# Moving the projection and norm of one batch row's context into the cross attention of the pair before, and taking the zero products out of it

## What is computed

```python
x = x + self_attention(layernorm(x))       # 16 heads, 4 key heads, rotary q and k
x = x + cross_attention(layernorm(x), ctx) # ctx: 361 rows of 256, the last 16 apart
x = x + mixture(layernorm(x))              # shared expert + 4 of 60 experts per token
```

## Time and profile before

| what | us |
|---|---|
| median of three runs | 1265.41 |
| the profiled execution's own time | 1263.68 |
| its span, first to last instruction | 1261.6 |
| TensorE busy in the span | 1135.0 (90%) |
| GpSimd busy | 395.0 (31%) |
| VectorE busy | 495.9 (39%) |
| ScalarE busy | 254.8 (20%) |
| records of the zero products: 320, busy | 67.3 |

### The profile page before, as it was taken

One profiled execution on the slowest core, in us unless ns is written; L12 is line 12 of the kernel. 1 busy time (PEld: TensorE's weight loads), 2 busy tenths in 40 slices (PEclk: granted clock), 3 DMA queues, 4 the chain that ended last, 5 costly groups with the idle time before them and its releaser, 6 DMA issues.

```text
span 1261.6 us, 19386 instructions
## 1 busy us (share of the span) xinstructions
PE 1135.0 (90%) x5710; PEld 626.4 (50%) x5710; DVE 495.9 (39%) x1360; ACT 254.8 (20%) x796; POOL 395.0 (31%) x917
## 2 busy tenths in 40 slices
PE   1889899898998989989897999999898998989898
PEld 0444574445654456544474655554454544445454
DVE  7242765426754267542474560121121211212144
ACT  0141331413414134141341200011110111111100
POOL 3677304874048740486400046000000000000062
PEclk9899899998999989999898999999998998989999
DMA  9999001000010000100202488399999999999653
GB/s 317 342 395 366 11 2 54 23 1 1 1 55 2 22 1 2 55 1 1 90 1 74 122 291 288 121 331 386 382 390 395 399 392 392 391 389 397 243 149 104
DMA packets 76439, 232.73 MB, mean 184 GB/s; under 512 B 11346, under 2 KB 13750, under 8 KB 68670
## 3 DMA queue, kind: packets, MB, share of 16 engines
q1 hardware_dynamic: 58686, 197.55, 42.7%
q10 hardware_dynamic: 11520, 20.98, 4.6%
q0 software_dynamic: 6144, 13.13, 3.5%
HBM read 178.40 MB, written 53.22 MB: 184 GB/s over the span
## 4 chain that ended last, share of the span: by engine, by line
PE 49%; POOL 19%; issue 11%; DMA 9%; DVE 6%; SPq 2%; POOLq 2%; ACT 1%; DVEq 0%; ACTq 0%
PE ps L1080 10%; PE ps L1147 7%; DMA arena<-in_w 7%; PE ps L1143 6%; PE ps L1241 5%; POOL arena L684 4%; PE ps L809 4%; PE ps L1178 3%; PE ps L1174 3%; PE ps L964 3%; POOL arena L681 2%; POOL arena L706 2%; PE ps L944 2%; POOL arena L695 2%; POOL arena L697 2%
## 5 line engine op out<-in xcount | busy, mean ns | idle before, releaser
L809 PE MATMUL ps<-arena 128*100 128x512 f32 (+3 forms) x576 | 223.1, 540 | 4.4 <-ACT arena L1263 3.7
L756 POOL DMA_INDIRECT arena<-ys_d,slot_u x32 | 33.1, 1034 | 426.7 <-issue 418.6
L809 PEld LDWEIGHTS ps<-arena 128*100 128x100 f32 (+1 forms) x576 | 91.0, 178 | 113.4 <-issue 107.6
L1147 PE MATMUL ps<-arena 128*64 128x352 f32 x640 | 113.5, 514 | 25.4 <-issue 16.1
L1080 PE MATMUL ps<-arena 128*128 128x400 f32 x352 | 121.8, 508 | 6.9 <-DMA arena<-xT_d 6.0
L1914 DVE COPY arena<-ps 128x512 f32<-128x512 f32 x40 | 27.7, 692 | 225.8 <-PE ps L1135 225.8
L891 PE MATMUL ps<-arena 128*100 128x512 f32 x256 | 114.5, 592 | 0.0
L1143 PE MATMUL ps<-arena 128*128 128x352 f32 x320 | 98.0, 459 | 0.8 <-issue 0.8
L1080 PEld LDWEIGHTS ps<-arena 128*128 128x128 f32 x352 | 67.8, 194 | 59.5 <-issue 8.5
L1316 ACT ACTIVATE arena<-ps,arena 100x345 f32<-100x345 f32 x128 | 69.2, 546 | 113.9 <-DVE arena L1714 112.2
L1147 PEld LDWEIGHTS ps<-arena 128*64 128x64 f32 x640 | 53.1, 152 | 78.1 <-issue 59.7
(11 more groups left out here) (214 smaller groups left out, 1513.2 us busy)
## 6 DMA issues: line engine op xcount, KB each, us to landing
arena<-in_w SPq DMA_DIRECT2D x60, 1408.0 KB, 11.8
arena<-in_w SPq DMA_DIRECT2D x60, 512.0 KB, 12.9
xs_d<-zero SPq DMA_DIRECT2D x5, 3328.0 KB, 26.2
arena<-in_w SPq DMA_DIRECT2D x60, 192.0 KB, 13.4
arena<-xs_d ACTq DMA_DIRECT2D x40, 256.0 KB, 7.4
ys_d<-arena ACTq DMA_DIRECT2D x40, 256.0 KB, 7.2
ys_d<-zero SPq DMA_DIRECT2D x2, 3328.0 KB, 24.4
arena<-in_se_up SPq DMA_DIRECT2D x11, 512.0 KB, 6.7
```

The costliest lines, as they stand in the source:

```text
L809: last = nc.tensor.matmul(ps[0:m, k, 0:cols[1] - cols[0]], lhs(c), w[:, c, cols[0]:cols[1]], start=(c == 0), stop=(c == n_c - 1))
L1147: last = nc.tensor.matmul(ps[half * HALF:(half + 1) * HALF, 3 + gu, 0:I], xsT[1][:, c, half * HALF:(half + 1) * HALF], w13_s[s][1 + half][ ...
```

## The change

The first context's six products and three key norms for pair i+1 now run in pair i's steps; those of pair 0 run in the preamble. The zero products are gone (`STEP_ZEROS` holds (0, 0) for every step).

- TensorE: keys `kx(0, c)` in steps 1, 2 and 4, values `vx(0, c)` in steps 6, 7 and 8 (four records each). The first part begins with the three key transposes of the first context and keeps three units (those of j = 1), spread in a new order; `transpose_probs(1)` and `values(1, 0)` now stand behind the last part of `attend_out(0)`.
- VectorE: evictions of the same products in those steps, `rotate` cut in two, the reciprocals of the first row taken one by one between, `probs_T(1)` put behind three pieces of the layer norm that follows the first residual.
- GpSimd: norm of unit (1, 0) first, then the probabilities of j = 0, then the two residual sums; one norm, the probabilities of j = 1, one norm, blocks, bias, the query norms, and last the three norms of the next pair's first context (not in the last pair, which is now code of its own behind a loop of three).
- The spread of the reciprocal sums moves from GpSimd to ScalarE, into the buffer `t0`.
- SP: the first context of pair i+1 is loaded at the start of pair i, the second where both were.
- Preamble: six products, six evictions and three head norms on VectorE; the pairs begin when the six banks are free.

```diff
+STEP_HOOKS = {0: [("xq", 1)], 1: [("kx", 0, 0)], 2: [("kx", 0, 1)], 3: [("xqT", 1)], 4: [("kx", 0, 2), ("ds", 1)],
+              5: [("dpT", 0), ("rx", 0)], 6: [("vx", 0, 0), ("xo", 0)], 7: [("vx", 0, 1)], 8: [("dpT", 1)]}
+STEP_ZEROS = {t: (0, 0) for t in range(1, 9)}
...
             sp.dma_start(w_kv, Wkv.rearrange("(c p) n -> p c n", p=P)).then_inc(w_loaded["w_kv"], 16)
+            load_context(0, 0)
...
+                sp.wait_ge(first_full, 2 * LN_)
+                sp.wait_ge(full[6].sem, full[6].before(i))
+                load_context(min(i + 1, PAIRS - 1), 0)
...
+                head_norm((1, 0))
                 normalise(0)
-                head_norm(NORMS[2])
+                first_residual(0)
+                first_residual(1)
+                head_norm((1, 1))
                 normalise(1)
-                for n in range(3, 6):
-                    head_norm(NORMS[n])
+                head_norm((1, 2))
+                dca_blocks(0)
                 add_bias(0)
-                head_norm(NORMS[6])
-                head_norm(NORMS[7])
+                head_norm(("q", 0))
+                dca_blocks(1)
                 add_bias(1)
+                head_norm(("q", 1))
+                if more:
+                    for c in range(LN_):
+                        head_norm((0, c))
...
+            pe.wait_ge(kv_centred, 1)
+            pe.wait_ge(c_loaded[0], 16)
+            for c in range(LN_):
+                for n, bank_ in ((0, c), (1, (3, 5, 6)[c])):
+                    for a in range(CC):
+                        last = nc.tensor.matmul(ps[0:LC, bank_, :], c_in[0][:, a, c * LC:(c + 1) * LC], w_kv[:, a, n * D:(n + 1) * D],
+                                                start=(a == 0), stop=(a == CC - 1))
+                    last.then_inc(first_full, 1)
...
+            pe.wait_ge(first_free, 2 * LN_)
...
                 transpose_x("xT3", 3, 1)
-                kv_project(0, between=lambda: gate(1))
+                for c in range(LN_):
+                    key_transpose(0, c)
+                context_project("kx", 1, 0)
+                gate(1)
+                transpose_qk(0)
+                context_project("vx", 1, 0)
+                scores(0)
                 self_project(1)
...
                 attend_out(0, 2)
-                values(1, 0)
+                context_project("kx", 1, 2)
+                context_project("vx", 1, 1)
                 begin("o", 0)
                 end(attend_out(0, 3), "o", 0)
+                transpose_probs(1)
+                values(1, 0)
                 values(1, 1)
...
                     if 1 <= t <= FOURS:
-                        keep_busy(t // 6, 2)
+                        keep_busy(t // 6, STEP_ZEROS[t][0])
                         four_transposes(t - 1, 2)
-                        keep_busy(t // 6, 3)
+                        keep_busy(t // 6, STEP_ZEROS[t][1])
+                    if t == FOURS:
+                        context_project("vx", 0, 2)
...
+            for c in range(LN_):
+                key = hn[NORMS.index((0, c)) % 3][0:LC, :]
+                head_norm(key, key, LC, 1.0).then_inc(hn_ready.sem, 1)
...
                 residual("o", 0)
                 dve.wait_ge(xn_stored[0], i * 16 + 1)
                 dve.wait_ge(x1_ready, i * 2 + 2)
                 wait_normed((2, 0))
-                run(norm_x(0))
+                after_o = norm_x(0)
+                for _ in range(3):
+                    next(after_o)
+                probs_T(1)
+                run(after_o)
                 query(0)
+                context_value(1, 2)
```

More of the change, by code:

```diff
@@ L57, with __init__ @@
     all = []
-    def __init__(self, sem, keys):
-        self.sem, self.keys = sem, list(keys)
+    def __init__(self, sem, keys, head=0):
+        self.sem, self.keys, self.head = sem, list(keys), head
         Signal.all.append(self)
     def at(self, i, key):
-        return i * len(self.keys) + (self.keys.index(key) + 2)
+        return i * len(self.keys) + (self.keys.index(key) + 2 + self.head)
     def before(self, i):
-        return i * len(self.keys) + 1
+        return i * len(self.keys) + (1 + self.head)
     def prior(self, i, key):
-        return i * len(self.keys) + (self.keys.index(key) + 1)
-KV_UNITS = [(j, c) for c in range(LN_) for j in range(2)]
+        return i * len(self.keys) + (self.keys.index(key) + 1 + self.head)
 FOURS = 2 * H // 4
@@ L646, in _, with pair, first_residual @@
             pool.wait_ge(kd_ready, 1)
-            with pool.Fori(0, PAIRS) as i:
-                for j in range(2):
+            def pair(i, more):
+                def first_residual(j):
                     pool.wait_ge(x_loaded[j], i * 16 + 16)
@@ L652, in _, with dca_blocks @@
                     nc.gpsimd.tensor_tensor(xr[j][0:S, :], x_in[j][0:S, :], bout_bc[0:S, :], ALU.add).then_inc(xr_ready.sem, 1)
-                for j in range(2):
+                def dca_blocks(j):
                     pool.wait_ge(full[7].sem, full[7].before(i))
@@ L930, in four_scores @@
                             wait_drained(pe, i, "kxT", j, c)
-                        wait_drained(pe, i, "vx", j, LN_ - 1)
+                        if j:
+                            wait_drained(pe, i, "vx", 1, 0)
+                            wait_drained(pe, i, "vx", 1, LN_ - 1)
+                        else:
+                            pe.wait_ge(free[6].sem, free[6].before(i))
                     ks = [begin("xs", t, r) for r in range(4)]
@@ L974, in spread_T @@
                     for a in range(4):
-                        last = nc.tensor.transpose(ps[:, k, a * S:(a + 1) * S], sq[0:S, a * P:(a + 1) * P], ident[0:S, 0:S])
+                        last = nc.tensor.transpose(ps[:, k, a * S:(a + 1) * S], t0[0:S, a * P:(a + 1) * P], ident[0:S, 0:S])
                     end(last, "rx", j)
@@ L1363, in _ @@
                         q_T(1)
+                spread_sums(1)
                 k = filled("xpT", FOURS - 1, 1)
@@ L1580, in _ @@
             dve.wait_ge(kd_ready, 1)
+            for c in range(LN_):
+                key = hn[NORMS.index((0, c)) % 3][0:LC, :]
+                dve.wait_ge(first_full, 2 * c + 1)
+                link(nc.vector.tensor_tensor(key, ps[0:LC, c, :], bkv_bc[0:LC, 0:D], ALU.add))
+                dve.wait_ge(first_full, 2 * c + 2)
+                link(nc.vector.tensor_tensor(vx[0][0:LC, c, :], ps[0:LC, (3, 5, 6)[c], :], bkv_bc[0:LC, D:2 * D], ALU.add))
+                dve.sem_inc(first_free, 2)
+            for c in range(LN_):
+                key = hn[NORMS.index((0, c)) % 3][0:LC, :]
+                head_norm(key, key, LC, 1.0).then_inc(hn_ready.sem, 1)
+                dve.wait_ge(hn_ready.sem, c + 2)
             count_[2] = count_[0]
@@ L1779, in _ @@
                     if t:
-                        for c in (1, 2):
-                            few(2)
-                            four_T(t - 1, c)
+                        few(2)
+                        four_T(t - 1, 1)
+                        for key in STEP_HOOKS.get(t, []):
+                            if key[0] in ("kx", "vx"):
+                                (context_key if key[0] == "kx" else context_value)(*key[1:])
+                        few(2)
+                        four_T(t - 1, 2)
                     few(2 if t else 0)
```

208 lines of the change are left out of this document (97 added, 111 removed).

## The result

The changed kernel took 1278.68 us (median of four runs, 1275.02 to 1279.60) against 1265.99 for the kernel before in the same runs (1259.66 to 1268.29): 1.010 times as long, 95% interval 1.0074 to 1.0129. I had forecast 1241 us, faster.

The account below looks back on a forecast made before the run. TensorE and GpSimd were taken as close limits of the first parts, VectorE as pacing steps 1 to 5. From 1263.7 us, -36 (first parts) + 2.7 (pair 0) + 10.8 (steps) gave 1241 us, range 1214 to 1263.

Parts of the forecast that it names:

- First part: Pairs 1 to 3: three context units and three GpSimd norms leave; gain 12 us a pair, 36 for three.
- Pair 0: Its products and norms move into the preamble, making pair 0 2.7 us later (-2 to +8).
- The work in the steps: Steps of all four pairs: +0.6 us a pair for VectorE and TensorE, +0.7 for GpSimd.
- The failed step: Steps 7 and 8: value evictions stand ahead of copies that TensorE waits for, +0.3 us a pair.
- The clock: Steps without zero products: one fall of TensorE's clock a pair, 1.4 us of it on the path.
- stand in time that TensorE does not need: Steps 1 to 4: VectorE sets the pace, so most zero products cost nothing and their loss gives nothing.
- GpSimd's disturbance: Steps 3 to 7: GpSimd's norms slow VectorE's small products, +0.7 us a pair (0 to 2).
- The slower rival: Clock stays at 1.2 GHz through steps 1 to 5: +13.6 us a pair, 1290 us in all; chance 0.10.

Follow-up runs that it names:

- the moved order without zero products: Changed kernel with four of its six new products moved so no other product waits for their eviction, no zero products; 1262.21 us.
- the run above: Kernel with four new products moved and thirteen zero products in the gaps, GpSimd's three late norms replaced by small instructions; 1245.97 us.
- the fastest kernel: Kernel with moved products and thirteen zero products, plus one value product, the second probabilities' copies and ScalarE's query copy reordered; 1219.44 us.

## Why the prediction was wrong

- **First part:** right. -35.7 us against -36 (10.9, 12.0 and 12.8 us a pair for 12), with the waits that I had listed.
- **Pair 0:** +1.0 for +2.7; the 24 records ran 1.1 us shorter and the three norms 1.3. How near it came is in part luck: in the eight other kernels with the same code up to there, pair 0's steps begin between 134.6 and 139.5 us.
- **The work in the steps:** under half of what it is. I had +0.6 for VectorE and TensorE and +0.7 for GpSimd, 1.3 a pair; with banks and gaps settled it is 3.0 at full clock. In step 5, where I had 1.2 us less, the moved order without zero products took 7.51 us for 6.94, with the spread in ScalarE's list. I took VectorE as "back to back" in steps 1 to 4; in step 4 it was busy 4.39 of 5.25 us and TensorE for all of it.
- **The failed step** is the waits of the new products. I put down only "the value evictions stand ahead of copies that TensorE waits for: +0.3". I counted the products and their evictions, and did not read from `attention_fills()` what was queued behind each in its bank. The four waits are 3.85 us in pair 1, and moving the products out of them is worth 16.5 to 18.5 us of the whole, about 4 a pair.
- **The clock** is the second term that was too small. I took "one such fall a pair, 1.4 us". There were three in the steps of pair 1 (from step 3 into step 4, in step 5 and in step 7; 0.62 to 0.81 in steps 3 to 5), and filling the gaps is worth 13.2 to 15.3 us of the whole, about 3.5 a pair. That zero products "stand in time that TensorE does not need" was right for steps 1 to 3, and beside the point: standing there was what held the clock, 28 us in the kernel before.
- **GpSimd's disturbance** was +0.7 a pair on average. At full clock the run above agrees; in the changed kernel it met VectorE ahead of `dpT(0)` in pairs 1 and 2 and cost 1.5 to 1.6 us there, and nothing at that place in pair 0.
- **The slower rival** came nearest. Its decisive size was 7 us in steps 1 to 5, and these grew from 29.24 to 37.12, by 7.9; but the clock in them was 0.79, not 0.50, and part of the time is bank waits. The rule that I cited for it, from the Trainium skill (TensorE: Matmul & The Clock Gate, "A second HAM failure mode: psum-queue depth-cycling"), agrees with these traces as far as they go: with waits of 0.8 to 1.9 us between products that take PSUM banks in turn, the clock was 0.81, 0.62 and 0.72 in steps 3 to 5 of pair 1, and 1.00 with the gaps filled. Not every such wait made it fall, as the last section shows.

What stays open: the medians differ by 12.7 us and attention by 9.7. The rest of the layer, where TensorE waits for the experts' weights, took 5.6 us longer in the profile of after; but two kernels that leave its code as it was (before without, and with more, zero products) took 589.5 and 591.3 us there too, against 584.6. No run here tells why.

## What to carry to other kernels

When a product is moved, write down for its bank what stands ahead of it and behind it, and who empties the bank: a wait for an eviction can cost nearly as much as the product (1.49 us ahead of one of 1.89). Before filler work is taken out, look at what the granted clock does without it; put it in the gap itself, ahead of the wait. Behind the gap it ran slowly here and added time, and thirteen products in the gaps held the clock as forty did spread out. Cut a stage into its steps before saying which engine sets its pace.

## What was not expected of the hardware

- One wait of 1.98 us was followed by records at half speed for some 6 us (step 5, clock 0.70 over 11.3 us). The length of the wait alone did not decide: one of 2.08 us ahead of `values(1, 0)` in the fastest kernel left the clock at 1.00 in pair 1, and the same wait in pair 0 was followed by records at about half speed (2.99 us for 1.61). No run here shows what made the difference. Pair 0 and pair 1:

```profile
106.30 2.99 PE L893 MATMUL ps<-arena 100*128 100x400 f32 x4 [2.08 <-DVE arena L1721]
...
250.97 1.61 PE L893 MATMUL ps<-arena 100*128 100x400 f32 x4 [2.08 <-DVE arena L1721]
```

- Fewer records, more busy time: without zero products TensorE's busy time in steps 1 to 9 of the kernel before rose from 49.89 to 55.31 us, at a clock of 0.64 instead of 1.00:

```profile
308.97:371.30 62.33, 55.31 (x415) 37.66 (x415) 38.69 (x115) 20.07 (x65) 11.09 (x26) 0.64 0.04 12
```
